# Order of the high and low products in the gate and up projections of a mixture-of-experts kernel (one Trainium2 core)

## The reference

```
H, I, CAP = 1024, 384, 256
inp = xin[:, :CAP]                          # [64, 256, 1024], gathered tokens
h   = silu(einsum('ech,ehi->eci', inp, wg)) * einsum('ech,ehi->eci', inp, wu)
out = einsum('eci,eih->ech', h, wd)
```

## Time and profile before

| | |
|---|---|
| time, median of 3 runs | 2393.93 us (2393.78 to 2395.6) |
| span of the profiled execution, first to last instruction | 2381.5 us |
| median less this span | 12.4 us |
| PE busy / weight load busy | 2354.5 us / 2074.8 us |
| DVE / ACT / POOL busy | 1664.0 / 1369.5 / 1414.4 us |
| experts (up and down) | about 188 us to 1774 us of the span |

### The profile page before, as it was taken

How to read it: one execution, slowest core, us unless ns; L and a number is a source line. 1 busy time by engine, 2 the same in 40 slices (tenths; PEclk the granted TensorE clock), 3 DMA queues, 4 the chain that set the end, 5 groups by cost and what they waited for, 6 DMA issues and landing times.

```text
span 2381.5 us, 35318 instructions
## 1 busy us (share of the span) xinstructions
PE 2354.5 (99%) x12762; PEld 2074.8 (87%) x12762; DVE 1664.0 (70%) x2874; ACT 1369.5 (58%) x2256; POOL 1414.4 (59%) x1032
## 2 busy tenths in 40 slices
PE   8989999999999999999999999999999999999999
PEld 5778888888888888888888888888889999999999
DVE  6888888888888878888888788888862244444443
ACT  5767777777767767777777777777761211111110
POOL 4027888787778777777777777777710122222222
PEclk9999999999999999999999999999999999999999
DMA  9998999999998999989989989899876354444441
GB/s 343 385 328 283 285 291 272 288 282 287 278 298 279 284 282 280 281 277 287 282 274 288 284 276 282 275 290 280 274 196 132 87 140 130 130 130 130 128 121 60
DMA packets 250352, 582.33 MB, mean 245 GB/s; under 512 B 82745, under 2 KB 106682, under 8 KB 250178
## 3 DMA queue, kind: packets, MB, share of 16 engines
q1 hardware_dynamic: 183202, 401.18, 51.5%
q0 software_dynamic: 55584, 160.02, 26.0%
q10 hardware_dynamic: 11392, 18.88, 2.2%
HBM read 456.51 MB, written 123.45 MB: 244 GB/s over the span
## 4 chain that ended last, share of the span: by engine, by line
PE 93%; POOL 2%; DMA 2%; issue 1%; DVE 1%; ACT 0%; ACTq 0%; SPq 0%; DVEq 0%; POOLq 0%
PE ps L808 25%; PE ps L821 21%; PE ps L920 17%; PE ps L807 12%; PE ps L878 5%; PE ps L804 4%; PE ps L677 2%; PE ps L913 2%; PE ps L805 2%; POOL Xg L573 1%; PE ps L687 1%; PE ps L893 1%; DMA Xg<-yd,idx 1%; PE ps L700 1%; PE ps L699 0%
## 5 line engine op out<-in xcount | busy, mean ns | idle before, releaser
L808 PE MATMUL ps<-XX,HR 128*128 128x512 f32 x2688 | 961.0, 397 | 0.0
L573 POOL DMA_INDIRECT Xg<-yd,idx x504 | 663.4, 1316 | 160.5 <-issue 152.7
L807 PE MATMUL ps<-XX,LR 128*128 128x256 f32 x2688 | 751.2, 279 | 0.1
L1540 DVE TENSOR_TENSOR LR<-raw,HR 128x1536 fp32r<-128x1536 f32 x384 | 657.3, 1752 | 3.7 <-ACT HR L1075 3.6
L808 PEld LDWEIGHTS ps<-XX,HR 128*128 128x128 f32 x2688 | 505.9, 188 | 104.4
L1075 ACT ACTIVATE HR<-raw 128x1536 fp32r<-128x1536 f32 x384 | 556.5, 1478 | 11.8 <-DMA raw<-in_L_ffn_wd 8.9
L807 PEld LDWEIGHTS ps<-XX,LR 128*128 128x128 f32 x2688 | 508.3, 189 | 18.3 <-DVE LR L1540 0.7
L595 POOL DMA_INDIRECT accd<-ot,toki x128 | 253.0, 1977 | 149.9 <-ACT ot L1129 127.7
L920 PE MATMUL ps<-MH,xT 128*128 128x392 f32 x1536 | 335.8, 344 | 0.0
L821 PE MATMUL ps<-LR,hH 128*128 128x512 f32 x768 | 303.3, 395 | 0.0
L821 PE MATMUL ps<-HR,hH 128*128 128x512 f32 x768 | 299.8, 390 | 2.9 <-DVE LR L1540 2.2
(11 more groups left out here) (214 smaller groups left out, 3226.1 us busy)
## 6 DMA issues: line engine op xcount, KB each, us to landing
raw<-in_L_ffn_wd SPq DMA_DIRECT2D x128, 768.0 KB, 4.8
raw<-in_L_ffn_wg SPq DMA_DIRECT2D x126, 768.0 KB, 7.3
raw<-in_L_ffn_wu SPq DMA_DIRECT2D x126, 768.0 KB, 6.9
yd<-yrow ACTq DMA_DIRECT2D x32, 512.0 KB, 6.7
x<-accd SPq DMA_DIRECT2D x32, 512.0 KB, 5.2
out<-osb SPq DMA_DIRECT2D x31, 512.0 KB, 3.0
xt<-in_x SPq DMA_DIRECT2D x25, 512.0 KB, 8.2
accd<-xt SPq DMA_DIRECT2D x25, 512.0 KB, 6.6
```

The lines of the kernel that those rows point to most:

```text
L573: eng.indirect_dma_start(Xg[:, c, q, :], None, yd4, bass.IndirectOffsetOnAxis(ap=idx4[:, e % 4, i:i + 1], axis=0))\
L807: eng.matmul(bank(out, 0, CAP), wl, xx[:, 0:CAP], start=False, stop=False)
L808: mm = eng.matmul(bank(out), wh, xx, start=False, stop=(k == 7))
L1540: eng.tensor_tensor(LR[:, (n + 2) % NHL, :], raw[:, n % NRAW, :], HR[:, (n + 2) % NHL, :].bitcast(F32), ALU.subtract).then_inc(s_L, 1)
```

## The change

From stretch 2 of each expert on, every k has H first and then L, where before k = 1 to 7 had L first. Stretch 1 keeps its order. The numbers, sizes and operands of the products stay. The last product of a block, which raises `s_up`, is now an L.

```diff
-                            if k == 0:
-                                eng.matmul(bank(out), wh, xx, start=True, stop=False)
-                                eng.matmul(bank(out, 0, CAP), wl, xx[:, 0:CAP], start=False, stop=False)
+                            if k == 0 or (b, g) != (0, 0):
+                                eng.matmul(bank(out), wh, xx, start=(k == 0), stop=(k == 7))
+                                mm = eng.matmul(bank(out, 0, CAP), wl, xx[:, 0:CAP], start=False, stop=(k == 7),
+                                                skip_group_check=(k == 7))
                             else:
                                 eng.matmul(bank(out, 0, CAP), wl, xx[:, 0:CAP], start=False, stop=False)
                                 mm = eng.matmul(bank(out), wh, xx, start=False, stop=(k == 7))
```

## The result

The changed kernel is slower: 2400.69 us (2398.51 to 2403.6, 7 runs) against 2392.98 us (2392.25 to 2395.6, 7 runs of the kernel before). The ratio is 1.0033 with a 95% interval of 1.0024 to 1.0042. The forecast was 2401.1 us, +0.30%.

A forecast was written before the change was run, and what follows sets the result against it. TensorE's own rhythm bounds the kernel; 60 experts x 0.12 us = 7.2 us lift the span from 2381.5 to 2388.7, and 12.4 us more give 2401.1 us (+0.30%), range 2392 to 2404.5.

The forecast's parts named there:

- The bound: In the steady experts only TensorE's product rate counts: busy without a gap from 273 to 1774 us, 25.02 us an expert.
- The sum: Experts 4 to 63 at 0.12 us each give 7.2 us; experts 0 to 3 taken as 0; 2401.1 us, +0.30%.
- Two rhythms as a state of TensorE: Gate and up pairs take 347 or 353 ns; the rhythm lasts through alternation and changes at seams between stretches.
- (b): Seams between stretches: only 1 to 2 keeps H, H, none has L, L; stretches 2 to 6 long, 0.12 us more an expert.
- the long rhythm: H and L pairs of a stretch at 353 ns, durations all 0.28 and 0.40; taken for stretches 2 to 6, 14.13 us.
- theory A: Expectation for experiments 2 and 3: only two wide products together turn the rhythm; experts at 24.88 and 24.91 us.
- The sign that I used: Seam into stretch 2: L805 at 0.28, next start 0.12 later, looks long before the second L; speaks for H, H as cause.
- (c): Stretch ends: `down` now follows an L and ACT's eviction waits for an L; costed at nothing, `down` left at 8.24 us.
- third rival: `down` hands over in another state, so stretch 1's 7 kept pairs get long too: +2.8 us, 2403.9 us; chance 0.07.
- The 12.4 us: Median of the runs above the profiled span of 2381.5 us; the same was added to the forecast span of 2388.7 us.

The follow-up runs named there:

- experiment 2: The changed kernel with H first in stretch 1 as well; ratio to the kernel before 1.0029 (1.0018 to 1.0039).
- Experiment 6: The changed kernel with every narrow product reading the high weights and token columns 256 to 511; only traced, experts at 25.14 us.
- Experiment 7: Kernel before, experts 4 to 57 in threes: fixed order (24.91 us), one of 18 stretch-1 orders (24.90 to 24.92 or 25.18 to 25.19), order of before; only traced.
- 9: Kernel before with H first everywhere except k = 3, 4 of stretch 1 and k = 2 to 7 of stretch 6; 2373.67 us, ratio 0.997.
- experiment 3: The changed kernel with stretch 2 also in the order of before, H first only from stretch 3 on; ratio to the kernel before 1.0027.
- experiment 1: The kernel before again, no edit, for a second profile; median 2381.36 us (2377.97 to 2387.4).
- 4: Each stretch with eight high products first, then eight low ones, against the kernel before; ratio 0.9997 (0.9986 to 1.0008).
- 10: The changed kernel again, no edit, on another chip; 2389.52 us, ratio to the kernel before 1.004 (1.0026 to 1.0053).

## Why the prediction was right, and where it was not

- **The bound.** TensorE's rate and nothing else: right. No kernel of the study has a wait of TensorE in the steady experts, and the interval repeats to 0.01 us wherever order and hand-over do. The granted clock is 1.00 there. For experts 0 to 3 I named only waits. In the kernel before, stretch 5 of expert 3, behind the wait of 1.8 us, took 4.44 us with TensorE busy throughout, at a granted clock of 0.62. The sum takes these experts as unchanged and does not suffer from it.
- **Two rhythms as a state of TensorE, kept while H and L alternate.** Right. Stretches 2 to 6 of the change are 40 pairs in one rhythm, and a quick expert of experiment 2 has 48. Experiment 6 excludes the operands. Experiment 7 shows that it is no chance: 18 equal cases, 18 equal times. Experiments 7 and 9 have the same instructions in both rhythms, so the flags of the products, the bank and the product that raises `s_up` are excluded as well; what is left is what ran before. There are three rhythms and not two, but two of them cost the same.
- **(b), which rhythm.** The choice was right, the price was right (0.12 us an expert, 25.14 us), but the reason was only half right. I took H, H for what brings in the long rhythm and L, L for idle. Here, from the short rhythm, H, H is indeed enough. But the long rhythm comes without either behind some hand-overs (experiment 2), and leaving it took more than the H, H (experiment 3): at a seam of before it was the two together. A meeting of two equal widths shifts the state, and its effect depends on the state it finds. Had I priced experiments 2 and 3 by that reason, as theory A did, I would have forecast two faster kernels, and both were slower. The sign that I used did not carry the choice. I read a long rhythm from L805 with 0.28 and a next start 0.12 us later. The seam into stretch 3 of the same expert shows the same, and stretch 3 is short:

```profile
703.94 0.28 PE L805 MATMUL ps<-XX,LR 128*128 128x256 f32 x1
704.06 0.27 PE L807 MATMUL ps<-XX,LR 128*128 128x256 f32 x1
```

  Only the row behind it differs, 0.27 here and 0.28 at the seam into stretch 2, and that is already the second L. In ns the distance behind L805 at the seam into stretch 2 is 113, which the short rhythm has as well. So the choice came out right on a sign that could not tell the two apart, which is in part luck.
- **(c), the ends.** Right: `down` stayed at 8.24 us and no wait came up. That `down` carries a state was in the third rival (stretch 1 getting long) and did not come true for this order; experiment 2 shows that it can.
- **The sum.** 7.2 us forecast, 7.7 measured between the medians. The 12.4 us that I put around the span were wrong: 1.7 lie around it (experiment 1). So the profiled execution of before took about 2383 us, 9 us less than the quickest of the timed ones (2392.25). Its expert 0 starts at 161.38 us, as on the quicker chips of experiments 1 to 4, 9 and 10; on which chip it ran is not known, so chip or chance stays open. It did no harm because only the difference was added to the median, but a comparison of spans would have given 15.3 us, twice the truth.
- **A price by width alone.** The Trainium skill (TensorE: Matmul & The Clock Gate, Back-to-back issue gap) gives an isolated gap of N / 2.4 + 2.5 ns at the full clock, and says that in a stream of weight loads and products both set the spacing, with about 131 ns for 512 columns. The traces here agree with neither: in the steady experts a product of 512 columns takes 224 to 242 ns from start to start and one of 256 columns 112 to 122. Six orders of the same products gave 24.91, 24.99, 25.02, 25.13, 25.14 us and a cycle around 25.10. In this kernel the order is worth up to 0.9% of an expert, which no price by width alone can give.

## What to carry to other kernels

When one engine bounds a stage, look whether equal stretches of it take equal times; where they don't and the times repeat exactly, the order of its own instructions may be the lever, and no wait will show it. The gain is small: 0.3% of this kernel. Don't reason from a rule for the order: try many orders inside one kernel, one in each iteration, read the interval of each from the trace, and choose one that is quick and hands over to itself. And compare steady intervals, not spans, for effects of a few us.

## What the runs showed of the hardware

A product's distance to the next depends on the history of products, in a way that repeats to a ns over 58 experts. By the start times in ns in the traces (finer than the printed rows), alternation of 512 and 256 columns has three stable forms. The long one repeats after three pairs (118, 241, 120, 236, 113, 232 ns from start to start, 1060 together, 353 a pair). One short one repeats after two pairs (112, 233, 117, 231: 693, 347 a pair), and the other, which is that of the quick experts, after a single pair (230 and 117, 347 a pair). `down`, 512 columns throughout, repeats after three products (226, 229, 232), grouped wide products of the up stage settle at 227 and grouped narrow ones at 120. What in TensorE carries the state, for instance how a weight load lies against the products beside it, was not tried and stays open. So does whether the forms are the same for other widths.
